# Two-layer cross-attention and expert kernel: front with shared row scaling and VectorE's second norm, experts by token half, third norm spread under other work

## The reference, cut to what matters

```python
x = x + xattn0(layernorm(x), ctx)    # softmax over a 256x256 score per batch, then a 512->128 product
x = x + moe(layernorm(x))            # 8 experts: h = silu(x W1) * (x W2), y = h W3; top-2 weights per row
x = x + xattn1(layernorm(x), ctx)    # 16 heads of 8 features, W_q, W_k, W_v, W_o
x = x + fp8ffn(layernorm(x))         # quantised 128x128 product and a bias
```

## Time and profile before

| | us |
|---|---|
| three runs: median (lowest to highest) | 235.59 (235.07 to 237.67) |
| the profiled execution, its time | 232.66 |
| its span, first to last instruction | 230.8 |
| PE busy | 191.4 (83% of the span) |
| DVE busy | 167.9 (73%) |
| ACT busy | 139.8 (61%) |
| POOL busy | 122.8 (53%) |

### The profile page before, as it was taken

The page is one execution under the profiler, slowest core; times in us unless marked ns, Lnnn a source line. Parts: engine busy times, 40 slices in busy tenths (PEclk is TensorE's granted clock), DMA queues, the critical chain, the costliest instruction groups (busy, mean ns, idle before and its releaser), DMA issues.

```text
span 230.8 us, 4208 instructions
## 1 busy us (share of the span) xinstructions
PE 191.4 (83%) x1178; PEld 147.3 (64%) x1178; DVE 167.9 (73%) x404; ACT 139.8 (61%) x264; POOL 122.8 (53%) x139
## 2 busy tenths in 40 slices
PE   5858884996979999999985889999999999886320
PEld 4645782655768888888865667776867776654220
DVE  3775774177768787887858898888978978735664
ACT  2282845946546556555584259887968769573452
POOL 4368648982967998989965322322313222203512
PEclk9999998599999999999999589999999999999755
DMA  6990220200843633642400000000000000000002
GB/s 234 384 390 18 90 96 0 91 0 9 257 115 131 227 100 127 227 149 86 128 3 0 0 0 0 6 0 3 0 3 0 0 0 1 0 3 0 0 0 91
DMA packets 8561, 17.13 MB, mean 74 GB/s; under 512 B 1242, under 2 KB 4187, under 8 KB 8291
## 3 DMA queue, kind: packets, MB, share of 16 engines
q1 hardware_dynamic: 6960, 16.03, 19.8%
q10 hardware_dynamic: 1586, 0.93, 1.3%
HBM read 10.11 MB, written 0.56 MB: 46 GB/s over the span
## 4 chain that ended last, share of the span: by engine, by line
PE 66%; DVE 12%; ACT 7%; issue 5%; POOL 4%; DMA 3%; SPq 0%; DVEq 0%; POOLq 0%; ACTq 0%
PE bank L1283 7%; PE bank L1068 6%; PE banks L1302 6%; PE bank L1070 6%; PE bank L1069 6%; PE bank L1314 5%; PE banks L1068 4%; PE banks L1070 4%; PE banks L1069 4%; DMA wxs<-wx 3%; PE bank L1082 2%; POOL att L283 2%; PE banks L1076 2%; PE bank L1291 2%; PE bank L1335 1%
## 5 line engine op out<-in xcount | busy, mean ns | idle before, releaser
L321 POOL TENSOR_TENSOR hids<-attT,hids 128x512 fp32r<-128x512 f32 x32 | 40.7, 1294 | 11.6 <-ACT hids L517 11.6
L934 DVE TENSOR_REDUCE negm<-bank 128x2 f32<-128x512 f32 x64 | 42.1, 688 | 5.0 <-PE bank L1283 3.5
L364 POOL TENSOR_TENSOR wx<-raw,const 32x256 fp32r<-32x256 f32 x32 | 19.5, 608 | 44.6 <-DVE raw L924 37.3
L575 ACT ACTIVATE raw<-banks 128x1024 f32<-128x1024 f32 x32 | 32.5, 1022 | 2.7 <-PE banks L1302 2.5
L861 DVE SCALAR_TENSOR_TENSOR att<-att,bank 128x512 f32<-128x512 f32 x32 | 22.0, 687 | 14.3 <-ACT att L510 14.1
L517 ACT CAST hids<-attT 128x512 fp32r<-128x512 f32 x32 | 19.8, 622 | 13.8 <-PE banks L1070 11.6
L1283 PE MATMUL bank<-wx 128*128 128x512 f32 x64 | 26.0, 450 | 2.5 <-DVE wx L944 1.4
L510 ACT ACTIVATE att<-bank 128x512 f32<-128x512 f32 x32 | 19.0, 598 | 13.0 <-PE banks L1070 10.5
L1068 PE MATMUL bank<-xT,wxs 128*128 128x512 f32 x48 | 20.1, 419 | 1.6 <-DMA wxs<-wx 1.6
L1070 PE MATMUL bank<-xT,wxs 128*128 128x512 f32 x48 | 19.4, 404 | 0.0
L1069 PE MATMUL bank<-xT,wxs 128*128 128x512 f32 x48 | 19.3, 403 | 0.0
(11 more groups left out here) (222 smaller groups left out, 466.4 us busy)
## 6 DMA issues: line engine op xcount, KB each, us to landing
wxs<-wx SPq DMA_DIRECT2D x8, 512.0 KB, 4.7
rwb<-routing SPq DMA_DIRECT2D x8, 512.0 KB, 4.3
raw<-in_w SPq DMA_DIRECT2D x1, 2048.0 KB, 11.7
wxs<-wx SPq DMA_DIRECT2D x8, 256.0 KB, 4.4
raw<-in_w SPq DMA_DIRECT2D x1, 1024.0 KB, 10.8
xs<-in_x SPq DMA_DIRECT2D x2, 256.0 KB, 3.1
ctxT<-in_ctxT SPq DMA_DIRECT2D x1, 512.0 KB, 4.6
ctx<-in_ctx SPq DMA_DIRECT2D x1, 512.0 KB, 5.9
```

The costliest lines, as they stand in the source:

```text
L321: pool.tensor_tensor(hids[:, p, 1, k, :], hid[:, k, :], plain(hids[:, p, 0, k, :]), ALU.subtract).then_inc(S["hid_lo"], 1)
L364: pool.tensor_tensor(km[rows, g, j, :], ks[rows, g % 2, :], const[rows, C_ZERO:C_ZERO + 1].broadcast_to([QUAD, SEQ]), ALU.add)\
L575: act.activation(probs[:, g % 2, 2 * r:2 * r + 2, :, :].rearrange("p h k q -> p (h k q)"), pair[r][:, :], ACT.Exp, scale=ATT_SCALE).then_i ...
L934: dve.tensor_reduce(negm[:, g % 2, r // 2, c0:c0 + QUAD + 1:QUAD], bk[1 + r % 2][:, :].rearrange("p (h k) -> p h k", h=2), AX.X, ALU.max, ...
```

## The change

Row scaling of the attention is shared: of each batch's two tiles DVE scales one and POOL the other, now as a two-input product with the row factor broadcast. POOL adds the bias `bl` to `xs` (two halves, early) instead of DVE. ACT keeps `cT`'s first half. `contexted(0)` comes directly after `queried(0)`. The scratch `ke` of the fp8 weight lies in PSUM. The second norm is scaled by DVE, half by half, and POOL holds its weight work back until that is done. PE's warm-up has 4 matmuls instead of 6.

Experts run by token half: units 0 to 7 are experts 0 to 7 on rows 0 to 511, units 8 to 15 on rows 512 to 1023. PE reads the weights where they are (`wx`), so SP's staging is gone; units are written out, without a loop. Routing is done per half: half 0 around up(1), half 1 at n = 3. The routing rows are spread in 4 transfers of two experts per half. `hid` has two buffers. The first half's sum is turned back at n = 10, added at n = 11, its third-norm moments taken at n = 12, POOL makes its factors at n = 12, ACT scales its tiles at n = 14 and 15. The second half's sum is turned in four parts, and added, normed and turned during batch 0 of the second attention. SP writes the zeros of `km` by a transfer.

```diff
-WARM_UP = 6
+WARM_UP = 4
...
-        rwb = sb("rwb", [P, 2, TOK])
+        rwb = sb("rwb", [P, E, HALF])
...
+            def spread(h, q):
+                src = rw_d[2 * q:2 * q + 2, h * HALF:(h + 1) * HALF].unsqueeze(0).broadcast_to([P, 2, HALF])
+                sp.dma_start(rwb[:, 2 * q:2 * q + 2, :], src).then_inc(S[f"rwb{h}{q}"], 16)
...
+            pool.wait_ge(S["ld_bl"], 16)
+            for h in range(2):
+                tiles = slice(*HALVES[h])
+                pool.wait_ge(S["ln1"], HALVES[h][1])
+                pool.tensor_tensor(xs[:, tiles, :], xs[:, tiles, :],
+                                   bl[:, :].unsqueeze(1).broadcast_to([P, TPH, P]), ALU.add)\
+                    .then_inc(S["bl_added"], 1)
...
+                pool.tensor_tensor(att[:, t, :], att[:, t, :], rinv[:, t:t + 1].broadcast_to([P, SEQ]), ALU.mult)\
+                    .then_inc(S["s_norm2"], 1)
...
-            w12_lo(0, 1, 2, 3, 4, 5)
-            negative_mean(0, HALVES[0])
-            w12_lo(6)
-            negative_mean(1, HALVES[1])
-            w12_lo(7)
+            w12_lo(0, 1, 2, 3, 4)
+            for h in range(2):
+                inverse_deviation(2, h, HALVES[h])
+            pool.wait_ge(S["ln2"], NT)
+            w12_lo(5, 6, 7)
...
+                dve.tensor_scalar(att[:, TPB * b, :], att[:, TPB * b, :], rinv[:, TPB * b:TPB * b + 1], None, ALU.mult)\
+                    .then_inc(S["s_norm"], 1)
...
+            for n in range(2, UNITS):
+                up(n)
+                down(n - 2)
+                if n == 2:
+                    pe.wait_ge(S["xT_lo"], 2)
+                    logits(1)
+                if n == 3:
+                    logits_turned(1)
+                if n == 4:
+                    weights_turned(1)
+                if n == UNITS - 6:
+                    first_half_turned()
...
+            for n in range(2, UNITS):
+                hidden(n)
+                if n == 3:
+                    routing(1)
+                weigh(n - 2)
+                if n == UNITS - 5:
+                    add_experts(0)
+                if n == UNITS - 4:
+                    sum_moments(0)
...
-            queried(0)
-            queried(1)
             for h in range(2):
+                queried(h)
                 contexted(h)
```

More of the change, by code:

```diff
@@ L223, in spread @@
[L223 to L234, removed]
@@ L591, in act_batch @@
                     exps(m, g, 0, first and g < 2)
+                    if first and g >= 2:
+                        later_norm_hi(g)
                     if g == 2 and not first:
@@ L857, in hidden @@
+                dve.tensor_tensor(rw[:, tiles, :], route[:, 0, tiles, :], route[:, 1, tiles, :], ALU.add)\
+                    .then_inc(S["route_s"], 1)
+            def hidden(n):
+                p = n % 2
                 for k in range(HB):
                     dve.wait_ge(S["tanh_s"], HB * n + k + 1)
-                    if not first:
+                    if n > 0:
                         dve.wait_ge(S["hid_s"], HB * (n - 1) + k + 1)
@@ L1200, in up @@
+            def up(n):
+                h, e = n // E, n % E
+                pe.wait_ge(S["w12_lo"], e + 1)
                 cols = slice(h * HALF, (h + 1) * HALF)
                 x = (xT[:, 0, cols], xT[:, 1, cols])
-                for k in blocks:
+                for k in range(HB):
                     for w, used in enumerate(("gate_s", "hid_s")):
-                        if not first:
+                        if n > 0:
                             pe.wait_ge(S[used], HB * (n - 1) + k + 1)
@@ L1221, in down, with first_half_turned, second_half_part @@
                 ins.then_inc(S["y_ps"], 1)
+            def first_half_turned():
+                pe.wait_ge(S["y_acc"], added(E - 1))
+                for t in range(TPH):
+                    ins = pe.transpose(bk[6][:, t * P:(t + 1) * P], accT[:, t * P:(t + 1) * P], ident)
+                ins.then_inc(S["accT_ps"], 1)
+            def second_half_part(src, first=False, last=False):
+                for t in range(TPH):
+                    ins = pe.matmul(bk[7][:, t * P:(t + 1) * P], src[:, t * P:(t + 1) * P], ident,
+                                    start=first and t == 0, stop=last and t == TPH - 1)
+                if last:
+                    ins.then_inc(S["accT_ps"], 1)
@@ L1236, in _ @@
[L1236 to L1252 removed]
+            logits(0)
@@ L1356, in pe_batch @@
                     shifted_scores(m, g, 1, first and g == 0)
+                    if first and g >= 2:
+                        pe.wait_ge(S["o_ev"], g - 1)
+                        for t in range(TPB):
+                            pe.wait_ge(S["ln3"], TPB * g + t + 1)
+                            ins = pe.transpose(bk[7][:, t * P:(t + 1) * P], xn[:, TPB * g + t, :], ident)
+                        ins.then_inc(S["x3T_ps"], 1)
                     if last and g == G - 1:
```

547 lines of the change are left out of this document (270 added, 277 removed).

## The result

The changed kernel took 236.29 us in the median of 12 runs (235.22 to 239.88), the kernel before 234.76 on the same chips: a ratio of 1.0078, interval 1.0044 to 1.0112. It is slower by 0.8%, where 235.2 and a hair faster (0.9985) had been forecast. That is inside the range and inside the 1% called "same", but on the other side of no change, and beyond the uncertainty of the measurement. Ratios here leave out the executions of a second, slower state, while medians in us take all, so the two can differ (half of best1's twelve executions ran in it, one of them at 457.47 us, which stays unexplained).

A forecast was written before the change was run, and what follows sets the result against it. PE was taken to bound units 6 to 15, so gains lay only at the seams. Terms 0 + 1.7 + 0.5 - 5.85 + 3.3 = -0.35 us against 232.66 gave 232.3, or 235.2 on the median; range 230.5 to 239.3.

The forecast's parts named there:

- Where two engines meet: Small DVE instructions with two SBUF inputs, or of the held kinds, wait for a running POOL instruction's end, up to 1.26 us.
- The first rival: POOL does not delay routing: half 0's ends at 50.8, 3.9 earlier; total -4.25, 231.3 us; chance 0.20.
- The front: Start to the first unit: gains and losses cancel, up(0) starts at 42.1, nothing won.
- Up(0) to up(6): First units with routing of both halves: up(6) starts 1.7 us late.
- up(3) starts at 60.4: After half 0's routing ends at 54.7, hidden(1), up(2), down(0) and half 1's logits precede up(3), at 60.4.
- up(6) starts at 75.1: After waits for half 0's weights and half 1's routing, up(6) starts at 75.1 instead of 73.39, 1.7 late.
- the rival of the transfers: Four 512 KB spreads served together: first lands at 67.5 instead of 62.2; +5, 240.6 us; chance 0.12.
- Units 6 to 15: Stretch from up(6) to down(14)'s end: bound by PE, which loses only 0.5 us to turning the first half's sum.
- the addition and moments sit in DVE's slack; 0: In units 6 to 15, addition (0.69) and moments (1.2) fit DVE's 0.85 us slack a unit, costing nothing.
- POOL's per-unit 3.9 stays: In units 6 to 15, POOL's work a unit remains 3.9 us and three of 14 sums fall away.
- Third norm: From down(14)'s end to first turned maxima: 11.5 us instead of 17.35, a gain of 5.85.
- Batch 0: First batch of second attention: added half-sum and norm work on DVE and ACT costs 3.3, 20.1 us instead of 16.8.

The follow-up runs named there:

- best1: Changed kernel with POOL's context part later, late norm's low parts behind maxima, half 0's sum turned a unit later, half 1's logits in PE's wait: 234.49 us, 0.9902.
- ctx_late: Changed kernel with POOL's low part of the context (2.4 us) moved behind the second unit's hidden parts: ratio 1.0007 to the kernel before.
- exp_only: Changed kernel with the old front (ACT's second norm, old order of POOL's weight parts): ratio 0.9963 to the kernel before.
- fill2: Changed kernel with 22 products nobody reads put between up(1) and the turning of the weights: ratio 1.0014 to the kernel before.
- turn_late: Changed kernel with the turning of half 0's sum and its addition one unit later: ratio 1.0041 to the kernel before.
- lo_early: Changed kernel with POOL's weight parts in the old order, not waiting for the second norm's end: ratio 1.0057 to the kernel before.

## Why the prediction was right or wrong

**Where two engines meet: right.** While POOL was busy, DVE's small two-input instructions, the cast and the `tensor_scalar` of routing each ended with a POOL instruction, and MAX8 (0.38 for four), the index searches (0.15 each) and the reciprocal (0.18) were not held. Routing of half 0 ended at 55.5, 54.7 predicted; counted from up(0) it was 12.3 and 12.6. By the rule of the Trainium skill (SBUF — State Buffer, Who interferes with whom) that is the port held as a lock, and this case's traces agree. The first rival, that POOL does not stand in the way, fell; ctx_late shows what one POOL instruction out of the way is worth, 1.7 us, and exp_only, which has the whole old front, 2.7.

**The front: within the 2 us allowed, and not knowable from one trace.** Nothing won or lost was forecast; +1.05 and -1.39 came, so that the two pairs average near zero is luck as much as working. Marks inside it came within 1.3 us: column product at 25.50 (25.9 predicted), first addition at 31.97 (30.7 predicted; the granted clock was 0.58 from 28 to 32), end of the second norm 41.1 (39.8). That the whole would scatter by 2 us with the clock stood nowhere. The medians (+1.5 to +1.8) lie 0.7 to 1.8 us below what the stretches behind up(0) give (+2.55 and +3.29), which would fit a new front that is some 1 us quicker on average; no run shows that by itself.

**Up(0) to up(6): the step "up(3) starts at 60.4", and with it "up(6) starts at 75.1", failed in size.** Predicted 33.0 us, measured 34.1 and 34.0. From the end of routing to up(3) 5.7 us were predicted and 6.8 measured. The wait for routing was there; what was left out is that PE came out of it at half clock for up(2), 1.1 us by fill2. The same price stood in the earlier trace rows, where the first product behind a wait took 0.77, and the prediction used it for the logits and not for up(2). From up(3) to up(6) it was 15.0 us, 14.7 predicted, although the 1.9 that weigh(0) was to wait did not come: the four spreads of 512 KB were issued from 58.70 on, landed 3.5 to 8.5 us after their issue, and DVE took half 0's weights at 62.37 straight behind its own work. They landed one after the other, so the rival of the transfers fell.

**Units 6 to 15: "the addition and moments sit in DVE's slack; 0" was right for DVE and the wrong engine.** The turning's 0.5 was there. But POOL, busy 39.22 of 42.97, has 0.4 us of slack a unit and got 2.0 in one piece, a term that "POOL's per-unit 3.9 stays" put at nothing, and PE asked for its sum a unit too soon. 2.0 instead of 0.5: 0.69 is the wait and its echo (turn_late), about 0.55 the gap in front of down(14), by the rows alone, and some 0.2 is not placed.

**Third norm: right,** 11.37 and 11.38 against 11.5, at full clock as put.

**Batch 0: right in size,** 20.3 against 20.1 forecast; the wait of 1.82 for ACT in it was not foreseen, as the sum there was by busy time and not by order, so part of the agreement is luck.

**The sum** thus missed by 1.1 (clock) and 1.5 (units 6 to 15, POOL's lag for the most part), 2.6 together, which on -0.35 makes 2.25: these two terms turned a forecast gain into a loss. The medians moved by 1.5 to 1.8, and the difference lies within what the front scatters.

## What to carry to other kernels

An engine's slack has to be counted for every engine that the added work touches, POOL's as well as DVE's, and at the unit where it is put, not over the stretch. Small DVE work with two inputs belongs where POOL rests; moving one POOL instruction of 2.4 us (1.7 us), or keeping the old front with its norm on ACT (2.7), was worth more than cutting the small work into pieces, which lost. A long wait of PE can cost more than itself, through the clock behind it. And before a front is judged by one trace of each kernel, trace each twice.

## What the runs showed of the hardware that was not expected

- The granted clock in the first 40 us differs between executions of one front: 1.00 in 14 to 32 us in one, 0.72 and 0.50 in parts of it in another, with PE's busy share about the same before the fall (5.42 and 5.39 of the first 8 us, 4.97 and 4.79 of the next 6). up(0) moves by 1.6 to 2.1 us between such executions, and the spread of one kernel's runs (232.7 to 237.7 for before) is of the same order or above. The Trainium skill (TensorE: Matmul & The Clock Gate, Part 1: The HAM clock gate) calls the number of products that run at the low clock variable from run to run of one kernel, for the start of a kernel; these traces show the like between 8 and 36 us, and at up(2), where the same program needed 6.06 us up to up(3) in after and 7.24 in turn_late. What decides it here stays open.
- Twenty-two products that nobody reads, put in a wait of 5.3 us, made the kernel 1.5 us faster (1.0014 beside 1.0078); twelve, with 2.67 us of wait left behind them, made no difference that can be told (1.0064).
- One POOL instruction after another can hold a single DVE group for 4.01 us (lo_early): four 128x128 scalings, of which the first three each end with a POOL part.
